# A decoder layer whose TensorE step puts one sequence's output projection ahead of another's transposes

## The reference

```python
x = layernorm(x + attn(x, ...))     # state-space mixer: in-projection, causal conv, silu,
                                    # FFT long convolution, gate by silu(z), out-projection 512 -> 256
x = layernorm(x + xattn(x, ctx))    # rmsnorm(x) @ W_x.T + b, plus a decaying scan over rmsnorm(ctx)
x = layernorm(x + ffn(x))           # router picks one of 8 experts per row: relu(x W1) W2
```

## Time and profile before

| | |
|---|---|
| median of 3 runs | 370.98 us (370.13 to 372.14) |
| the profiled execution | 371.73 us, its span 369.8 us |
| PE busy | 325.6 us, 88% |
| DVE busy | 211.4 us, 57% |
| POOL busy | 201.5 us, 54% |
| ACT busy | 151.8 us, 41% |
| L1336, the transposes of `x1_r` | 32, median 259 ns |
| L1347, the output projection | 128, mean 379 ns |
| L871, the copy of the transposes | 16, median 357 ns |

### The profile page before, as it was taken

How to read it: one execution, slowest core, us unless ns; L and a number is a source line. 1 busy time by engine, 2 the same in 40 slices (tenths; PEclk the granted TensorE clock), 3 DMA queues, 4 the chain that set the end, 5 groups by cost and what they waited for, 6 DMA issues and landing times.

```text
span 369.8 us, 6464 instructions
## 1 busy us (share of the span) xinstructions
PE 325.6 (88%) x1892; PEld 258.7 (70%) x1893; DVE 211.4 (57%) x439; ACT 151.8 (41%) x383; POOL 201.5 (54%) x321
## 2 busy tenths in 40 slices
PE   1999879999899999999987128999999999999980
PEld 1455436557677787778775127899999999999960
DVE  4999993525977687778742472244344434434431
ACT  2788845247443453354353100523422432342220
POOL 5789960325678658776762133055455554655652
PEclk9999989999999999999998655999999999999996
DMA  7900000512556656653640564001101100011110
GB/s 209 352 8 1 3 0 0 181 28 51 167 152 202 186 152 177 170 182 99 210 140 27 211 270 156 2 28 43 31 32 29 37 31 29 28 35 38 28 44 21
DMA packets 17030, 35.04 MB, mean 95 GB/s; under 512 B 3456, under 2 KB 8327, under 8 KB 16360
## 3 DMA queue, kind: packets, MB, share of 16 engines
q1 hardware_dynamic: 14840, 30.01, 25.7%
q0 software_dynamic: 1872, 4.59, 4.2%
q10 hardware_dynamic: 288, 0.07, 0.1%
HBM read 30.99 MB, written 4.20 MB: 95 GB/s over the span
## 4 chain that ended last, share of the span: by engine, by line
PE 76%; DVE 11%; POOL 3%; ACT 3%; DMA 3%; issue 2%; SPq 0%; DVEq 0%; POOLq 0%; ACTq 0%
PE ps L1417 18%; PE ps L1435 17%; DVE stage_b L957 7%; PE ps L1347 7%; PE ps L1327 7%; PE ps L1225 6%; PE ps L1272 4%; PE ps L1368 4%; PE ps L1273 3%; PE ps L1372 2%; DMA w<-in_x_t 2%; PE ps L1200 1%; PE ps L1404 1%; PE ps L1379 1%; DMA stage_b<-x_rows,stage_b 1%
## 5 line engine op out<-in xcount | busy, mean ns | idle before, releaser
L1417 PEld LDWEIGHTS ps<-stage_b 128*128 128x128 f32 x576 | 69.9, 199 | 2.6 <-DVE stage_b L1149 1.0
L1417 PE MATMUL ps<-stage_b 128*128 128x128 f32 x576 | 70.3, 282 | 1.2 <-ACT stage_b L900 1.2
L1435 PE MATMUL ps<-w,stage_b 128*128 x288 | 65.2, 380 | 1.1 <-DVE stage_b L1174 1.1
L1435 PEld LDWEIGHTS ps<-w,stage_b 128*128 128x128 f32 x288 | 53.3, 190 | 8.0 <-issue 1.5
L1008 DVE TENSOR_TENSOR stage_b<-ps,w 112x512 f32<-112x512 f32 x64 | 39.7, 683 | 23.5 <-PE ps L1273 21.4
L632 POOL TENSOR_TENSOR stage_b<-stage_b 112x512 f32<-112x512 f32 x16 | 21.4, 1339 | 44.5 <-DVE stage_b L1008 32.3
L900 ACT ACTIVATE stage_b<-ps 128x256 f32<-128x256 f32 x19 | 7.3, 385 | 85.0 <-PE ps L1404 85.0
L891 ACT ACTIVATE stage_b<-ps,b 128x128 f32<-128x128 f32 x144 | 39.2, 383 | 7.2 <-issue 7.2
L673 POOL DMA_INDIRECT stage_b<-x_rows,stage_b x21 | 31.4, 1496 | 9.7 <-issue 5.5
L1149 DVE COPY stage_b<-w 128x2048 f32 x19 | 24.2, 1275 | 21.3 <-issue 14.3
L1327 PEld LDWEIGHTS ps<-consts,stage_b 112*128 112x128 f32 x256 | 31.0, 192 | 7.1 <-issue 6.6
(11 more groups left out here) (164 smaller groups left out, 528.5 us busy)
## 6 DMA issues: line engine op xcount, KB each, us to landing
w<-in_w SPq DMA_DIRECT2D x16, 512.0 KB, 4.2
w<-in_w SPq DMA_DIRECT2D x16, 256.0 KB, 3.0
w<-in_w SPq DMA_DIRECT2D x4, 1024.0 KB, 8.8
stage_b<-in_ctx SPq DMA_DIRECT2D x16, 224.0 KB, 2.8
w<-in_x_t SPq DMA_DIRECT2D x4, 448.0 KB, 6.8
stage_b<-in_x SPq DMA_DIRECT2D x16, 112.0 KB, 3.0
x_rows<-stage_b SPq DMA_DIRECT2D x16, 112.0 KB, 1.9
w<-in_w_in SPq DMA_DIRECT2D x2, 512.0 KB, 5.6
```

The lines of the kernel that those rows point to most:

```text
L1417: last_ = m.matmul(ps[:, 2 * par + f // 4, (f % 4) * P:(f % 4 + 1) * P], w1_now[par][:, k, f * P:(f + 1) * P], rows_t[:, par, k * P:(k + 1 ...
L1435: last_ = m.matmul(ps[:, 4 + par, 0:D], h_t[:, par, f * P:(f + 1) * P], w2[:, e, f, :], start=(f == 0), stop=(f == FT - 1))
```

## The change

In TensorE's step, part 3 and part 4 trade places: the output projection of sequence s-2 is issued first, then the transposes of `x1_r` of sequence s-3. Instructions, tiles, banks, waits and semaphores are the same; no other engine's stream is touched.

```diff
-                b, par, half = seq(pair, q, 3)
-                if b is not None:
-                    pe.wait_ge(x1r_set, b + 1)
-                    need(pe, x1t_set, b)
-                    for k in range(DT):
-                        last_ = m.transpose(ps[:, 5, k * L:(k + 1) * L], x1_r[:, par, k * P:(k + 1) * P],
-                                            ident[0:L, 0:L])
-                    last_.then_inc(x1t_ps, 1)
-
                 b, par, half = seq(pair, q, 2)
                 if b is not None:
                     pe.wait_ge(gate_set, b + 1)
...
                     last_.then_inc(out_ps, 1)
+
+                b, par, half = seq(pair, q, 3)
+                if b is not None:
+                    pe.wait_ge(x1r_set, b + 1)
+                    need(pe, x1t_set, b)
+                    for k in range(DT):
+                        last_ = m.transpose(ps[:, 5, k * L:(k + 1) * L], x1_r[:, par, k * P:(k + 1) * P],
+                                            ident[0:L, 0:L])
+                    last_.then_inc(x1t_ps, 1)
```

## The result

| | median us | runs |
|---|---|---|
| before | 371.48 | 4 (370.13 to 372.14) |
| after | 377.21 | 4 (375.52 to 377.73) |

The ratio is 1.0136, with a 95% interval of 1.0108 to 1.0164, so the change costs 4.0 to 6.1 us. A second comparison, of 5 runs against 11, gave 1.0134 (1.0111 to 1.0157). I had forecast +5.7 us and 376.7 us. The profiled execution took 376.90 us and its span is 375.0 us, 5.2 more than before.

The account below looks back on a forecast made before the run. TensorE was taken to bound stage B's steps 4 to 15, without idle time. The terms +6.0, -0.25 and 0 gave +5.7 us after rounding, 376.7 us against the median of 370.98, range 374.0 to 379.0.

Parts of the forecast that it names:

- The sign that was named: End of stage B: L1368 of step 18 should stand about 5.7 us later than its 200.13.
- middle step: Stage B's steps 4 to 15: TensorE busy for all 7.30 us; 7.80 us forecast after the change.
- (a): Steps 4 to 15: ACT's copy L871 loses its cover, so L1368 waits 0.50 us a step, +6.0 us.
- (c): Step 3: the 1.22 us wait for L817 goes, but ACT's L871 doesn't move; -0.25 us, ends 0 and -1.2.
- (d): Steps 16 and 17: waits of 0.26 and 1.24 us go, but L1368's chain through L827 holds; 0, ends -1.5 and +0.5.
- (e): Behind stage B: the granted clock's fall or rise could shift time up to 3.2 us; 0 taken, 1.5 us kept each side.
- The rival that the loop's rests would make the clock fall: Loop: TensorE's 0.5 us rests drop the granted clock to 0.75; about 406 us; chance 0.04.
- The faster one: Stage B: copy covered in the loop, 2.7 us of waits in steps 3, 16, 17 gone; 368.3 us; chance 0.05.
- Partial hiding: Steps 4 to 15: the wait is only 0.13 to 0.25 us a step; 372.3 to 373.8 us; chance 0.07.
- Nothing moves: Whole kernel: the queue runs far enough ahead, or gains and losses cancel; 371.0 us; chance 0.04.

Follow-up runs that it names:

- ends: Against the kernel before: the output projection goes ahead of the transposes of x1_r only in steps 2, 3 and 16 to 19; ratio 0.9985.
- split2: Against the kernel before: two of the projection's four matmuls go ahead of the transposes of x1_r, two stay behind; ratio 0.9998.
- drain_swap: Kernel before, but from step 17 L1368 and L1372 go ahead of the x2 transposes on TensorE, L827 behind L871 on ACT; ratio 0.9945.
- split1: Against the kernel before: three of the projection's four matmuls go ahead of the transposes of x1_r, one stays behind; ratio 1.0034.
- cover_transform: Changed kernel with the next sequence's forward transform moved between the x2 transposes and L1368; ratio 1.0027 against before.
- drain_both: Kernel before, with the projection ahead of the x1_r transposes from step 16, and L1368, L1372 ahead of x2 transposes, L827 behind L871 from 17; ratio 0.9886.
- after_twice: Changed kernel with ACT copying the transposes of x1_r twice, first to a tile nobody reads; ratio 1.0258 against before.
- middle: Against the kernel before: the new order only in steps 4 to 15, the old one in step 3 and the drain; ratio 1.0185.

## Why the prediction was right

The medians differ by 5.73 us where 5.7 was forecast. That is closer than the reasoning reaches, and so in part luck: in the two profiles stage B takes 5.8 us more, and 0.8 us ahead of it and -1.4 us behind it, on which the forecast put nothing, partly cancel each other. What was right for its reasons is stage B. The sign that was named, L1368 of step 18 about 5.7 us later than 200.13, is such a mixture too: it stands at 206.71, 6.6 us later, of which 0.8 lie ahead of the stage.

**What bounds the kernel.** The reading that a middle step had no idle time of TensorE, so that no order could shorten it and each wait would lengthen it, held: `ends`, `split2` and `drain_swap` all have 7.30 us, none less, and each wait put in showed in full.

**(a) The copy's wait.** 0.50 us was placed from starts, and the steps lengthened by 0.50 to 0.51. Each part can be seen after: 0.60 us from load to copy (0.61 taken), 0.36 for the copy, 0.05 to the dependent load. The wait at L1368 is 0.47 us by its own note, under the 0.7 allowed. That it is the cover which counts, and neither the neighbourhood of the inverse transform nor the projection's early place, is shown by split1, split2 and cover_transform. That it is the copy's length is shown by the doubled copy. L1368's weight load itself starts 0.05 us behind the copy, in every step from 3 to 18 of the kernel after. So the load wasn't done while waiting, and the steps lengthened by 0.50 us, not by the 0.4 that the forecast drew from the Trainium skill's rule on weight loads pulled ahead ("TensorE: Matmul & The Clock Gate", Part 2). The 0.1 us itself was read from one kind of row: a first matmul stands 0.09 us behind its load at L1368 in step 8 of the kernel before (132.44 and 132.53), but 0.22 us at L1357 (132.12 and 132.34).

**(c) Step 3.** -0.25 us was forecast, and `ends` has -0.26. The wait of 1.22 us was gone, only 0.26 of it won, and as the forecast said L871 didn't move, since it stands behind L845: in the kernel after L1368 waits for L871 in its place.

```profile
96.20 0.37 ACT L845 ACTIVATE stage_b<-shared,stage_b 113x112 f32<-113x112 f32 x1
96.48 0.33 ACT L871 ACTIVATE stage_b<-ps 128x224 f32<-128x224 f32 x1
96.86 0.70 PEld L1368 LDWEIGHTS ps<-w_x,stage_b 128*112 128x112 f32 x4 [1.14 <-ACT stage_b L871]
```

**(d) The drain.** 0 was taken, with ends at -1.5 and +0.5. In step 17 of the kernel after, the projection started at 197.92 and no longer waited for L817, and L1368 came at 201.54, behind L827 and L845 as the forecast had it:

```profile
197.92 1.96 PE L1338 MATMUL ps<-w,stage_b 128*112 128x256 f32 x8
...
200.36 0.60 ACT L827 ACTIVATE stage_b<-stage_b 112x256 f32<-112x256 f32 x1 [1.12 <-POOL stage_b L655]
200.87 0.37 ACT L845 ACTIVATE stage_b<-shared,stage_b 113x112 f32<-113x112 f32 x1
...
201.01 0.20 PEld L1357 LDWEIGHTS ps<-consts,stage_b 112*128 112x128 f32 x2 [1.15 <-ACT stage_b L827]
...
201.15 0.33 ACT L871 ACTIVATE stage_b<-ps 128x224 f32<-128x224 f32 x1
...
201.54 0.70 PEld L1368 LDWEIGHTS ps<-w_x,stage_b 128*112 128x112 f32 x4 [0.32 <-ACT stage_b L871]
```

On TensorE the x2 transposes, which L1368 stands behind, wait for L827 as well. `ends` shows that this nets to nothing (its steps 16 to 18 are as long as before's), `drain_both` that removing the second obstacle frees the first one's win. One phrase of the forecast needs mending: it called the second norm's chain what held the drain. It is that chain only because ACT's and TensorE's queues put L871 and L1368 behind it; L1368 needs nothing of it.

**(e) The clock.** 0 was taken. Between the two profiles it gave back 0.36 us in the drain and 0.87 us in the first expert tile, 1.2 us together, inside the 1.5 kept for it. That its sign was for the changed kernel isn't the change's doing as far as is known: the same kernel once more (`after_again`) took 8.66 us instead of 9.61 in the drain and 6.70 instead of 5.85 in the tile. The rival that the loop's rests would make the clock fall did not come: the clock is 1.00 in the loop at 7.81 us and in `after_twice`'s at 8.05 us, whose step is 0.75 us over that of before. By TensorE's rows it rests 0.25 us in a step of the one and 0.50 in a step of the other. So what the Trainium skill's "TensorE: Matmul & The Clock Gate" says under "A second HAM failure mode: psum-queue depth-cycling", of short rests between groups of matmuls, didn't happen with rests of this size.

**The other rivals.** The faster one decided only if the copy had cover; where I gave it cover (split2, which keeps the win in step 3) the kernel was level with before, so its 2.7 us were never there: of the 1.22 us in step 3 only 0.26 came back, and of the waits in steps 16 and 17 nothing, since another chain ended almost as late at each. Partial hiding (0.13 to 0.25 us) is what split1 builds on purpose, at 0.07. "Nothing moves" is out by all runs.

## What to carry to other kernels

When an engine has no idle time in a loop, its order is still not free: between giving a result to another engine and needing it back there must lie at least the whole round trip (here 0.61 us from the transposes' load to the copy, 0.36 for the copy, 0.05 back), and moving the cover away cost what was missing, within 0.03 us, in every step. Before moving work ahead of a wait, ask what else holds the instruction behind it: in the drain the queues' order hid what the projection's early place could win: 0 and 1.0 us alone, 2.5 together. Such a win may be had where it is, by choosing the order by the step, with the loop left alone.

## What the runs showed that I hadn't expected

- The start of stage B lies anywhere from 89.54 to 91.91 us in 13 traces whose code ahead of it has the same instructions. In the two traces of the changed kernel it differs by 1.30 us, and so do the spans (375.0 and 376.3). So a change of half a microsecond is better read between two marks in the trace than from the median.
- Two ACT copies from PSUM of 0.36 us each, back to back, start 0.25 us apart, so the second costs 0.25 us on a path and not 0.36.
- The granted clock in the drain differs from trace to trace. The four matmuls of the last L1368 took 1.12 us at full clock (after_again, drain_both), 1.47 partly at half (after), and 2.05 at half (before, ends, middle). The same code, after and after_again, took 9.61 and 8.66 us from there to L1389, so it can lose about 1 us there or not. What decides it, no run shows.
